# A block of selective scan and FFN on one core: two loads change places, the opening's copies of B and C move to VectorE, and products, a row and an up projection get other slots

## The chip, the cores and the metric

One core of a Trainium2 chip runs the whole program. The metric is the device time of one execution in microseconds (us). The core has five engines that run their own instruction streams in order and meet through semaphores: PE (TensorE, matmuls; PEld is its weight load), DVE (VectorE), ACT (ScalarE), POOL (GpSimd) and SP (SyncE, which here only issues DMAs).

## The reference

```
mod = (silu(c) @ wmod).reshape(1, 6, 1, 256)            # sa, ca, ga, sb, cb, gb
ga, gb = sign(ga) * max(|ga|, 0.25), sign(gb) * max(|gb|, 0.25)
h = layernorm(x) * (1 + ca) + sa                        # x: 2048 tokens x 256
# selective SSM, 16 states n for each of 256 channels, token by token:
dt, B, C = split(h @ x_proj_w.T, [128, 16, 16])
delta = softplus(dt @ dt_proj_w.T + b);  A = -exp(A_log)
state[n] = exp(delta * A[n]) * state[n] + delta * B[n] * h
y = sum over n of state[n] * C[n] + D * h
x = x + ga * y
h = layernorm(x) * (1 + cb) + sb
g = (h @ gate_w.T) * gate_s;  u = (h @ up_w.T) * up_s     # 704 wide, ternary weights
x = x + gb * (((silu(g) * u) @ down_w.T) * down_s)
```

## The kernel before

**Tiling.** The 2048 tokens go in four chunks (c = 0 to 3) of 512. The 256 channels are two halves h of 128 partitions. Step c scans chunk c: 16 slots, one for each state row n, and at slot n the two halves are scanned by DVE (`scan`, L995). I write "scan 2.1" for row 2, half 1. Before a scan ACT makes its decay, exp(delta A), in one of two PSUM banks (`make_decay`, L830), so a decay can be made only when the scan two before it is done. POOL makes the drive of row n, u times B's row, three slots ahead (`drive`, L642); B's rows arrive in pairs in the tiles `brow`, by DMAs that repeat a row of a DRAM scratch (`bc_dram`) on all 128 partitions. Three `brow` buffers serve rows 0 and 1, 2 and 3, 4 and 5, and so on.

**Products.** The state of row n is multiplied by C's row n, one slot later. The table `POOL_C` says which rows POOL does (L654, C's row from a tile `crow` that a DMA filled); the others are DVE's (`times_c`, L969), and for these PE first repeats C's row on 128 partitions in the one PSUM bank `rows_ps` (`spread_row`, L1294). So row by row: DVE's product frees `rows_ps`, PE spreads the next row, DVE can multiply again. PE adds each product into `sums`, three slots behind the scan (`add_state`, L1320), and the D term first of all (`add_dterm`, L1306).

**Beside the scan.** While chunk c is scanned, "F" tasks prepare chunk c + 1 and "K" tasks run the FFN of chunk c - 1. F: statistics of x (st0, st1, agg on DVE), rstd on ACT, nmr (minus mean times rstd) on POOL, xn0 and xn1 on ACT (L713), transposes xT on PE (L1207), hmod0 and hmod1 on ACT (L728), z on PE (L1193), then abs, exp, zb and ln on ACT and delta on DVE; and bc, the product that gives B and C: ACT copies it to `bc_sb` (L752), from where SP stores it to `bc_dram`, and rounds C into `c_parts` (chi, L759), of which DVE takes the rest (clo, L901). K: x2 (`sums` added to x, L895), statistics, h2T, gate0 to gate4, mixed and up0 to up4 on PE (L1241), ACT's gates (L799), one silu over all gates with a table load at each end (L818 to L822), hdn5 and hdn0 to hdn4 on DVE (gates times ups, L942 and L953), and four downs (L1273). "S" tasks are set-up in the opening and in step 0: the last of them fill the weights' bias `wb` and scale the down weights.

**What sets the order.** Lists written by hand give each task a slot: (8.5, "F ln0") is slot 8, behind the second half; -3 means three slots before the step, 16 and over the next step. `FIRST` is for the opening (before step 0) and for chunk 0, `PLAN` for the middle, `CLOSING` for the FFN of chunk 2 during step 3, `FINAL` for that of chunk 3 behind the last scan. `SECOND_LATER` moves the F tasks of chunk 1, which would fall in the opening, by so many slots (2 where it names none). At each slot an engine does its scan, decay or drive, then the products, then its tasks; it never skips ahead, so a task that waits holds all behind it. `PLACE` and its kin give each PE result its PSUM bank; banks 0 to 2 are `side`, 3 is `rows_ps`, 4 and 5 are `decay`.

SP issues in the opening: x of chunk 0, the projection weights, then `load_more`: x of chunk 1 behind a wait for chunk 0's, the FFN weights, the rest of wmod. Behind that come, slot by slot, the stores and loads of B and C and a small DMA that keeps each state's last column.

## Time and profile before

| | |
|---|---|
| median of 3 runs | 316.56 us (315.71 to 316.79) |
| the profiled execution's own time | 314.61 us |
| its span, first to last instruction | 312.8 us |
| lies around the span | 1.8 us |
| DVE busy | 256.8 us, 82% |
| PE busy | 248.9 us, 80% |
| POOL busy | 227.0 us, 73% |
| ACT busy | 183.7 us, 59% |
| mean granted TensorE clock | 0.874 |

Stages of the span: up to 25.4 us the opening (no scan yet), then step 0 up to 84, step 1 up to 146.7, step 2 up to 209.0 and step 3 up to 273.7 us; the rest is the last chunk's FFN. The page divides the span into 40 slices of 7.8 us; each digit is a busy share in tenths, and for PEclk the granted clock in tenths of full speed. A timeline row reads: start (us), duration or, for xN instructions, the time from the first to the end of the last (us), engine, line, operation, written tile <- read tiles, shapes, count, and in brackets how long the engine sat idle just before and whose result ended that.

### The profile page before, as it was taken

How to read it: one execution, taken by the hardware profiler on the slowest of the kernel's cores; microseconds unless marked ns; L12 is line 12 of the kernel's file. 1: busy time of each engine (PE TensorE's matmuls, PEld its weight loads, DVE VectorE, ACT ScalarE, POOL GpSimd, SP SyncE). 2: the span in 40 equal slices, each digit the busy share in tenths (PEclk: the TensorE clock that was granted, in tenths of full speed). 3: DMA queues.
4: the chain of work that ended last, by engine and by line, in shares of the span. 5: the costliest groups of instructions: out<-in, count | busy, mean ns of one | idle time of the engine just before them, and what ended most of it. 6: DMA issues, size and time to landing. Idle time of an engine off the chain costs nothing. (4 is left out here: it accounts for less than half of the span.)

```text
span 312.8 us, 3793 instructions
## 1 busy us (share of the span) xinstructions
PE 248.9 (80%) x1226; PEld 185.5 (59%) x1226; DVE 256.8 (82%) x330; ACT 183.7 (59%) x294; POOL 227.0 (73%) x113
## 2 busy tenths in 40 slices
PE   7876799846387787848889997667899947897995
PEld 7634796435274455635658675446687835685874
DVE  3589966999999899969999999599988959944420
ACT  2688544765845976896349867932464883306400
POOL 1007789999999999979879997995599996700000
PEclk9995559997579889965999999958799995999999
DMA  7916897469262743392524735725636400001002
GB/s 249 327 48 162 156 143 203 69 104 233 73 133 72 137 103 107 72 147 28 124 69 108 161 90 118 135 38 151 167 90 149 118 1 0 2 0 67 2 0 71
DMA packets 33173, 33.09 MB, mean 106 GB/s; under 512 B 14912, under 2 KB 20224, under 8 KB 33152
## 3 DMA queue, kind: packets, MB, share of 16 engines
q1 hardware_dynamic: 32736, 32.01, 44.7%
q10 hardware_dynamic: 416, 0.81, 0.8%
q8 instruction: 12, 0.20, 0.3%
q14 instruction: 9, 0.07, 0.1%
HBM read 30.40 MB, written 2.36 MB: 105 GB/s over the span
## 5 line engine op out<-in xcount | busy, mean ns | idle before, releaser
L642 POOL TENSOR_TENSOR drv<-u,brow 128x1024 f32<-128x1024 f32 x63 | 147.8, 2362 | 21.0 <-DVE u L917 17.1
L830 ACT ACTIVATE decay<-delta,A 128x512 f32<-128x512 f32 x128 | 87.6, 688 | 82.9 <-DVE state L995 81.0
L995 DVE TENSOR_TENSOR_SCAN state<-decay,last,drv 128x512 f32<-128x512 f32 x96 | 119.1, 1268 | 11.7 <-ACT decay L830 11.4
L654 POOL TENSOR_TENSOR drv<-state,crow 128x1024 f32<-128x1024 f32 x29 | 68.7, 2369 | 9.9 <-DVE state L995 9.9
L1320 PE MATMUL sums<-ident,drv 128*128 128x128 f32 x512 | 72.1, 294 | 0.7 <-POOL drv L654 0.5
L1320 PEld LDWEIGHTS sums<-ident,drv 128*128 128x128 f32 x512 | 62.6, 151 | 12.0 <-issue 7.8
L969 DVE TENSOR_TENSOR drv<-state,rows_ps 128x1024 f32<-128x1024 f32 x35 | 41.8, 1195 | 5.4 <-PE rows_ps L1294 5.4
L1241 PE MATMUL side<-h_hi,ffn_hi 128*128 128x512 f32 x76 | 30.0, 479 | 18.6 <-DVE gates L942 16.1
L995 DVE TENSOR_TENSOR_SCAN state<-decay,drv 128x512 f32<-128x512 f32 x32 | 37.5, 1207 | 1.7 <-issue 1.1
L1294 PE MATMUL rows_ps<-c_parts,sel 64*128 64x512 f32 x35 | 19.6, 561 | 22.9 <-DVE drv L969 22.9
L1273 PE MATMUL side<-down_sb,gates 128*128 128x256 f32 x120 | 30.4, 403 | 4.3 <-DVE gates L953 3.5
L1273 PEld LDWEIGHTS side<-down_sb,gates 128*128 128x128 f32 x120 | 22.9, 199 | 10.3 <-issue 7.4
L1241 PEld LDWEIGHTS side<-h_hi,ffn_hi 128*128 128x128 f32 x76 | 14.5, 220 | 24.5 <-issue 23.0
L1241 PE MATMUL side<-h_lo,ffn_hi 128*128 128x512 f32 x76 | 26.5, 433 | 0.0
L1294 PEld LDWEIGHTS rows_ps<-c_parts,sel 64*128 64x128 f32 x35 | 7.2, 206 | 32.5 <-DVE drv L969 27.9
L1241 PEld LDWEIGHTS side<-h_lo,ffn_hi 128*128 128x128 f32 x76 | 16.4, 216 | 4.3
L799 ACT ACTIVATE gates<-side,wb,pack_sb 128x512 f32<-128x512 f32 x18 | 13.6, 768 | 3.3 <-PE side L1241 3.2
L1193 PE MATMUL side<-hmod,W_sb 128*128 128x512 f32 x24 | 11.0, 603 | 3.7 <-ACT hmod L728 3.7
L953 DVE SCALAR_TENSOR_TENSOR gates<-side,wb,gates 128x512 f32<-128x512 f32 x17 | 12.4, 736 | 1.5 <-PE side L1241 1.5
L1257 PE MATMUL decay<-down_sb,gates 128*128 128x256 f32 (+1 forms) x48 | 11.2, 387 | 0.0
L617 POOL TENSOR_TENSOR nmr_K<-negmean_K,rstd_K 128x4 f32<-128x4 f32 x4 | 0.8, 199 | 13.6 <-ACT rstd_K L706 13.6
L1306 PEld LDWEIGHTS sums<-diag_D,hmod 128*128 128x128 f32 x64 | 9.2, 225 | 1.7 <-issue 1.7
(142 smaller groups left out, 291.9 us busy)
## 6 DMA issues: line engine op xcount, KB each, us to landing
brow<-bc_dram SPq DMA_DIRECT2D x31, 512.0 KB, 5.5
crow<-bc_dram SPq DMA_DIRECT2D x13, 512.0 KB, 7.0
resid<-in_x SPq DMA_DIRECT2D x4, 512.0 KB, 5.4
out<-resid SPq DMA_DIRECT2D x8, 256.0 KB, 2.2
gates<-in_wmod ACTq DMA_DIRECT2D x1, 768.0 KB, 6.1
gates<-in_wmod SPq DMA_DIRECT2D x1, 768.0 KB, 8.7
last<-state SPq DMA_DIRECT2D x48, 1.0 KB, 2.5
crow<-bc_dram SPq DMA_DIRECT2D x3, 256.0 KB, 3.7
```

The lines of the kernel that those rows point to most:

```text
L642: nc.gpsimd.tensor_tensor(drv[j % RING_DRV][:, :, 0:S], u[:, c % 2, :, 0:S], b.unsqueeze(1).to_broadcast([P, HALVES, S]), ALU.mult).then_i ...
L654: nc.gpsimd.tensor_tensor(drv[j % RING_DRV][:, :, 0:S], state[j % RING_STATE][:, :, 0:S], row.unsqueeze(1).to_broadcast([P, HALVES, S]), A ...
L799: nc.scalar.activation(gates[:, j, 0:S], src[:, 0:S], ACT.Silu if c == NCH - 1 else ACT.Identity, bias=wb[:, j:j + 1], scale=pack_sb[:, CO ...
L830: nc.scalar.activation(decay[i % RING_DECAY][:, 0:S], delta[:, c % 2, h, 0:S], ACT.Exp, scale=A[:, h * N + n:h * N + n + 1]).then_inc(deca ...
L953: nc.vector.scalar_tensor_tensor(gates[:, j, 0:S], src[:, 0:S], wb[:, FULL + j:FULL + j + 1], gates[:, j, 0:S], ALU.add, ALU.mult).then_in ...
L969: nc.vector.tensor_tensor(drv[j % RING_DRV][:, :, 0:S], state[j % RING_STATE][:, :, 0:S], rows_ps[:, 0:S].unsqueeze(1).to_broadcast([P, HA ...
L995: nc.vector.tensor_tensor_scan(state[j % RING_STATE][:, h, 0:S], decay[i % RING_DECAY][:, 0:S], drv[j % RING_DRV][:, h, 0:S], before, ALU. ...
L1241: ins = nc.tensor.matmul(to[:, 0:S], weights, data, start=part is h2_hi and k == 0, stop=part is h2_lo and k == HALVES - 1)
L1257: ins = nc.tensor.matmul(to[:, b * D:(b + 1) * D], gates[part, j, rows], down_sb[part, j, :], start=j == FULL and b == 0, stop=j == FULL - ...
L1273: nc.tensor.matmul(to, gates[:, j, rows], down_sb[:, j, :], start=j == 0, stop=False)
L1294: nc.tensor.matmul(rows_ps[:, 0:S], sel[:, n:n + 1].to_broadcast([2 * 2 * N, P]), c_parts[:, c % 2, 0:S], start=True, stop=True).then_inc( ...
L1320: ins = nc.tensor.matmul(sums[:, b * D + h * P:b * D + (h + 1) * P], of[:, h, b * P:(b + 1) * P], ident[:, :], is_transpose=True, start=Fa ...
```

## The change

- **Loads.** SP issues the FFN weights ahead of x of chunk 1; the wait for chunk 0's x moves to the weights. DVE's `equal` (does rounding change the weights, L1081, three parts) waits for the first half of the rounded weights only in its first part.
- **Opening's copies.** For chunk 0 the copies bc and chi go from ACT to DVE. Chunks 1 to 3 keep them on ACT.
- **Statistics of x of chunk 1.** `SECOND_LATER` changes: st0, st1 and agg run in step 0 at slots 0.5, 1 and 1 instead of in the opening, rstd at 1.5 instead of 0.5, nmr at slot 2 instead of 0. xn0 and xn1 stay at slots 2 and 2.5.
- **Products.** In steps 1, 2 and 3 two DVE products are done at slots s and s + 0.5 of `SILU_SLOT` (13, 13, 10), for rows s - 2 and s - 1, and the second one's row is spread a slot later. POOL takes row 10 instead of 11 in step 1, and 11 instead of 8 in step 3; step 2 keeps its rows.
- **Step 3.** up2 of chunk 2 goes to slot 11 and to the bank `rows_ps`, up3 and up4 to banks 1 and 0, hdn2 and hdn3 half a slot up. Row 15 is spread at slot 13 (`LAST_ROW`), ahead of down0 and down1, behind a wait for up2's bank.

```diff
-POOL_C = [[4, 6, 9, 11, 13]] + [[1, 3, 5, 7, 9, 11, 13]] * (NCH - 3) + [[1, 3, 5, 6, 7, 10, 13]] + [[1, 2, 4, 5, 7, 8, 10, 12, 13, 14]]
+POOL_C = [[4, 6, 9, 11, 13]] + [[1, 3, 5, 7, 9, 10, 13]] * (NCH - 3) + [[1, 3, 5, 6, 7, 10, 13]] + [[1, 2, 4, 5, 7, 10, 11, 12, 13, 14]]
+SILU_SLOT = [None, 13, 13, 10]
 DVE_C = [[n for n in range(N) if n not in at] for at in POOL_C]
...
-SECOND_LATER = {"st0": -7, "st1": -7, "agg": -7}
+SECOND_LATER = {"st0": 3.5, "st1": 4, "agg": 3.5, "rstd": 3, "nmr": 4}
 FIRST = {
...
-        (7, "F clo"), (8, "F delta0"), (8, "F u0"), (8, "F drive0"), (9, "F delta1"), (9, "F u1"), (9, "F drive1"),
-        (6, "S equal"), (16.5, "S mod2"), (17.5, "S gb"), (22.5, "S wb"), (31, "S same"),
+        (6, "F bc"), (6, "F chi"), (7, "F clo"), (8, "F delta0"), (8, "F u0"), (8, "F drive0"), (9, "F delta1"), (9, "F u1"), (9, "F drive1"),
+        (5, "S equal"), (16.5, "S mod2"), (17.5, "S gb"), (22.5, "S wb"), (31, "S same"),
     ],
...
-        (4, "F abs0"), (4, "F exp0"), (4, "F zb0"), (5, "F bc"), (5, "F chi"), (6, "F ln0"), (6, "F abs1"), (6, "F exp1"), (7, "F zb1"), (7, "F ln1"),
+        (4, "F abs0"), (4, "F exp0"), (4, "F zb0"), (6, "F ln0"), (6, "F abs1"), (6, "F exp1"), (7, "F zb1"), (7, "F ln1"),
...
     "sync": [
-        (1, "S x"), (1, "S ffn"), (1, "S wmod"), (6, "F bc"), (20, "S down"), (26, "S xs"),
+        (1, "S ffn"), (1, "S x"), (1, "S wmod"), (6, "F bc"), (20, "S down"), (26, "S xs"),
     ],
...
-        (11.5, "K hdn5"), (11.5, "K hdn0"), (12, "K hdn1"), (12.5, "K hdn2"), (13, "K hdn3"), (13, "K hdn4"),
+        (11.5, "K hdn5"), (11.5, "K hdn0"), (12, "K hdn1"), (12, "K hdn2"), (12.5, "K hdn3"), (13, "K hdn4"),
...
-        (9, "K up0"), (10, "K up1"), (12, "K up2"), (12, "K up3"), (12, "K up4"),
+        (9, "K up0"), (10, "K up1"), (11, "K up2"), (12, "K up3"), (12, "K up4"),
...
-    "K up0": 0, "K up1": 2, "K up2": 1, "K up3": 0, "K up4": 2, "K down": (1, 2),
+    "K up0": 0, "K up1": 2, "K up2": 3, "K up3": 1, "K up4": 0, "K down": (1, 2),
 }
...
 PLACE_FIRST = {"F xT": (0, 1), "S mod": 3, "F z": (4, 5), "F bc": 2, "F sp": (0, 1)}
+LAST_ROW = 13
 LEAD = 3
...
                 yield kind, name, int(chunk)
+def product_slot(c, n):
+    if SILU_SLOT[c] is None or n not in (SILU_SLOT[c] - 2, SILU_SLOT[c] - 1):
+        return n + KEEP_LAG
+    return SILU_SLOT[c] + (0 if n == SILU_SLOT[c] - 2 else 0.5)
+def row_slot(c, n):
+    if (c, n) == (NCH - 1, N - 1):
+        return LAST_ROW
+    return n + (SILU_SLOT[c] is not None and n == SILU_SLOT[c] - 1)
...
                 elif name == "x":
-                    sp.wait_ge(x_loaded[0], 16)
                     load_x(1)
...
                 elif name == "ffn":
+                    sp.wait_ge(x_loaded[0], 16)
                     for m, w in enumerate((gateT, upT)):
...
                                             ALU.add).then_inc(x2_ready, 1)
+                elif name == "bc":
+                    src, i, k = side_bank(("F bc", c, 0))
+                    dve.wait_ge(side_full[i], k + 1)
+                    nc.vector.tensor_copy(bc_sb[:, 0:S], src[0:2 * N, 0:S]).then_inc(bc_ready, 1)
+                elif name == "chi":
+                    src, i, k = side_bank(("F bc", c, 0))
+                    nc.vector.tensor_copy(c_parts[0:2 * N, c % 2, 0:S], src[0:2 * N, 0:S]).then_inc(chi_ready, 1)
                 elif name == "clo":
...
-                    dve.wait_ge(ffn_hi_ready, HALVES)
                     for to, part in EQUAL:
+                        dve.wait_ge(ffn_hi_ready, 1 if part.stop <= 2 * INTER else HALVES)
                         nc.vector.tensor_tensor(equal_to(to, part), flat(ffn_hi)[:, part].bitcast(F32),
...
                             scan(step, n, h)
-                        for c, m in lagged(step, n, KEEP_LAG) if h == 0 else ():
-                            if m in DVE_C[c]:
-                                times_c(c, m)
+                        for c in (step - 1, step):
+                            for m in DVE_C[c] if 0 <= c < NCH else ():
+                                if c * N + product_slot(c, m) == step * N + n + h / 2:
+                                    times_c(c, m)
                         for task in side_tasks("vector", step, n + h / 2):
...
                     pe.wait_ge(side_free[i], k)
-                if i >= SIDE and use[0][0] == "K":
+                if i >= SIDE and use[0][0] == "K" and use[1] == NCH - 1:
                     pe.wait_ge(scan_done, UNITS * HALVES)
                     pe.wait_ge(prod_dve, rows_upto(NCH))
+                elif i >= SIDE and use[0][0] == "K":
+                    pe.wait_ge(prod_dve, rows_upto(NCH) - 1)
                 return to, side_full[i]
...
                     pe.wait_ge(prod_dve, before)
+                if (c, n) == (NCH - 1, N - 1):
+                    pe.wait_ge(*emptied(("K up2", NCH - 2, 0)))
                 if c == NCH - 2 and n >= BC_SLOT:
...
                 for n in range(N):
-                    spread = 0 <= step < NCH and n in DVE_C[step]
-                    follows = spread and (n - 1) % N in DVE_C[step - (n == 0)]
-                    if spread and not follows:
-                        spread_row(step, n)
+                    rows = [m for m in DVE_C[step] if row_slot(step, m) == n] if 0 <= step < NCH else []
+                    follows = bool(rows) and (rows[0] != n or (n - 1) % N in DVE_C[step - (n == 0)])
+                    if rows and not follows:
+                        spread_row(step, rows[0])
                     for task in side_tasks("tensor", step, n):
                         side_work(*task, full_weights)
-                    ending = step == NCH - 1 and n == N - 1
-                    if spread and follows and not ending:
-                        spread_row(step, n)
+                    if rows and follows:
+                        spread_row(step, rows[0])
                     for c, m in adds_at(step, n):
                         add_state(c, m)
-                    if ending and follows:
-                        spread_row(step, n)
```

On POOL, where the opening ends and step 0 begins; L642 and L659 are the drives of rows 1, 2 and on, L617 and L634 nmr of chunk 0 and then of chunk 1. Before:

```order
L617 TENSOR_TENSOR nmr_F<-negmean_F,rstd_F 128x4
L642 TENSOR_TENSOR drv1<-u,brow0 128x1024
L642 TENSOR_TENSOR drv2<-u,brow1 128x1024
L617 TENSOR_TENSOR nmr_F<-negmean_F,rstd_F 128x4
L642 TENSOR_TENSOR drv3<-u,brow1 128x1024
L642 TENSOR_TENSOR drv4<-u,brow2 128x1024
L642 TENSOR_TENSOR drv5<-u,brow2 128x1024
```

And after, at the same place of POOL:

```order
L634 TENSOR_TENSOR nmr_F<-negmean_F,rstd_F 128x4
L659 TENSOR_TENSOR drv1<-u,brow0 128x1024
L659 TENSOR_TENSOR drv2<-u,brow1 128x1024
L659 TENSOR_TENSOR drv3<-u,brow1 128x1024
L659 TENSOR_TENSOR drv4<-u,brow2 128x1024
L634 TENSOR_TENSOR nmr_F<-negmean_F,rstd_F 128x4
L659 TENSOR_TENSOR drv5<-u,brow2 128x1024
```

Chunk 1's nmr has moved behind the drives of rows 3 and 4, the second of which reads the third brow buffer.

On ACT, start of step 0, before: two decays of row 0, rstd of chunk 1 (L702 to L706), a sum of the weights' comparison (L695), the decays of row 1, and so on to xn0 and xn1 (L713).

```order
L830 ACTIVATE decay<-delta,A 128x512 x2
L702 ACTIVATE logvar_F<-meanvar_F,eps 128x4
L704 ACTIVATE negmean_F<-meanvar_F 128x4
L706 ACTIVATE rstd_F<-logvar_F 128x4
L695 ACTIVATE drv,same<-drv 128x1024
L830 ACTIVATE decay<-delta,A 128x512 x2
L695 ACTIVATE drv,same<-drv 128x1024
L830 ACTIVATE decay<-delta,A 128x512
L713 ACTIVATE xn_F<-resid,nmr_F,rstd_F 128x256 x2
L695 ACTIVATE drv,same<-drv 128x768
L830 ACTIVATE decay<-delta,A 128x512
L713 ACTIVATE xn_F<-resid,nmr_F,rstd_F 128x256 x2
```

And after:

```order
L847 ACTIVATE decay<-delta,A 128x512 x2
L712 ACTIVATE drv,same<-drv 128x1024
L847 ACTIVATE decay<-delta,A 128x512 x2
L719 ACTIVATE logvar_F<-meanvar_F,eps 128x4
L721 ACTIVATE negmean_F<-meanvar_F 128x4
L723 ACTIVATE rstd_F<-logvar_F 128x4
L712 ACTIVATE drv,same<-drv 128x1024
L847 ACTIVATE decay<-delta,A 128x512
L730 ACTIVATE xn_F<-resid,nmr_F,rstd_F 128x256 x2
L712 ACTIVATE drv,same<-drv 128x768
L847 ACTIVATE decay<-delta,A 128x512
L730 ACTIVATE xn_F<-resid,nmr_F,rstd_F 128x256 x2
```

rstd has moved behind the decays of row 1; xn0 still stands between the two decays of row 2, and xn1 ahead of those of row 3.

On PE in step 3, from the end of the ups: L1241 and L1270 are gates and ups, L1273 and L1274 (then L1302 and L1303) the downs, L1320 (L1351) the adds, L1294 (L1325) a spread row. Before:

```order
L1241 MATMUL side<-h_lo,ffn_hi 128x512 x2
L1320 MATMUL sums<-ident,drv 128x128 x16
L1273 MATMUL side<-down_sb,gates 128x256 x5
L1274 MATMUL side<-down_sb,gates 128x256
L1273 MATMUL side<-down_sb,gates 128x256 x5
L1274 MATMUL side<-down_sb,gates 128x256
L1320 MATMUL sums<-ident,drv 128x128 x8
L1294 MATMUL rows_ps<-c_parts,sel 128x512
L1320 MATMUL sums<-ident,drv 128x128 x32
```

And after:

```order
L1270 MATMUL side<-h_lo,ffn_hi 128x512 x2
L1351 MATMUL sums<-ident,drv 128x128 x8
L1325 MATMUL rows_ps<-c_parts,sel 128x512
L1351 MATMUL sums<-ident,drv 128x128 x8
L1302 MATMUL side<-down_sb,gates 128x256 x5
L1303 MATMUL side<-down_sb,gates 128x256
L1302 MATMUL side<-down_sb,gates 128x256 x5
L1303 MATMUL side<-down_sb,gates 128x256
L1351 MATMUL sums<-ident,drv 128x128 x40
```

Row 15 has moved ahead of the downs; five adds follow the downs as before.

## Rows read from the trace of the kernel before

**Rows 1.** The page: DVE and the rest over the span, granted clock in slices

```profile
PE 248.9 (80%) x1226; PEld 185.5 (59%) x1226; DVE 256.8 (82%) x330; ACT 183.7 (59%) x294; POOL 227.0 (73%) x113
...
PEclk9995559997579889965999999958799995999999
```

**Rows 2.** Timeline of ACT, opening and step 0

```profile
14.13 2.64 ACT L689 ACTIVATE ffn_hi<-ffn_sb 128x1408 fp32r<-128x1408 f32 x2 [0.88 <-DMA ffn_sb<-in_upT]
...
18.58 0.57 ACT L752 ACTIVATE bc_sb<-side 32x512 f32<-32x512 f32 x1
...
30.30 1.09 ACT L713 ACTIVATE xn_F<-resid,nmr_F,rstd_F 128x256 f32<-128x256 f32 x2 [0.24 <-POOL nmr_F L617]
...
32.13 0.67 ACT L830 ACTIVATE decay<-delta,A 128x512 f32<-128x512 f32 x1
32.74 1.08 ACT L713 ACTIVATE xn_F<-resid,nmr_F,rstd_F 128x256 f32<-128x256 f32 x2
...
41.56 0.76 ACT L728 ACTIVATE hmod<-side,gmod 128x512 f32<-128x512 f32 x1
...
52.02 0.69 ACT L765 ACTIVATE splus<-side,pack_sb 128x512 f32<-128x512 f32 x1 [3.62 <-PE side L1193]
```

**Rows 3.** Timeline of DVE, opening and step 0

```profile
16.80 3.23 DVE L1081 TENSOR_TENSOR drv<-ffn_hi,ffn_sb 128x1024 f32<-128x1024 f32 x3 [1.09 <-ACT ffn_hi L689]
...
20.35 0.68 DVE L901 TENSOR_TENSOR c_parts<-side,c_parts 32x512 fp32r<-32x512 f32 x1
...
35.05 2.33 DVE L995 TENSOR_TENSOR_SCAN state<-decay,drv 128x512 f32<-128x512 f32 x2
...
38.41 2.33 DVE L995 TENSOR_TENSOR_SCAN state<-decay,drv 128x512 f32<-128x512 f32 x2
43.10 1.22 DVE L969 TENSOR_TENSOR drv<-state,rows_ps 128x1024 f32<-128x1024 f32 x1 [2.36 <-PE rows_ps L1294]
```

**Rows 4.** DMAs issued from 22 to 23 us: size, us from issue to landing

```profile
crow<-bc_dram SPq DMA_DIRECT2D x1, 512.0 KB, 8.9
brow<-bc_dram SPq DMA_DIRECT2D x1, 512.0 KB, 12.6
```

**Rows 5.** Timeline of POOL, start of step 0: nmr, drive of row 3, row 4

```profile
30.07 0.20 POOL L617 TENSOR_TENSOR nmr_F<-negmean_F,rstd_F 128x4 f32<-128x4 f32 x1
30.22 2.36 POOL L642 TENSOR_TENSOR drv<-u,brow 128x1024 f32<-128x1024 f32 x1
34.91 9.30 POOL L642 TENSOR_TENSOR drv<-u,brow 128x1024 f32<-128x1024 f32 x4 [2.33 <-DMA brow<-bc_dram]
```

**Rows 6.** Timeline of PE, step 0: transposes xT, row 3, D term

```profile
37.17 1.97 PE L1207 MATMUL side<-ident,xn_F 128*128 128x128 f32 x8
...
42.27 0.79 PE L1294 MATMUL rows_ps<-c_parts,sel 64*128 64x512 f32 x1
42.99 3.62 PE L1306 MATMUL sums<-diag_D,hmod 128*128 128x128 f32 x16
```

**Rows 7.** Timeline of ACT ahead of silu, steps 1 and 2

```profile
128.82 0.69 ACT L830 ACTIVATE decay<-delta,A 128x512 f32<-128x512 f32 x1 [0.92 <-DVE state L995]
...
195.72 0.69 ACT L830 ACTIVATE decay<-delta,A 128x512 f32<-128x512 f32 x1 [0.50 <-DVE state L995]
```

**Rows 8.** Timeline of DVE: scans behind silu in steps 1, 2, 3; row 11's product

```profile
138.60 2.46 DVE L995 TENSOR_TENSOR_SCAN state<-decay,last,drv 128x512 f32<-128x512 f32 x2 [2.42 <-ACT decay L830]
...
202.75 2.46 DVE L995 TENSOR_TENSOR_SCAN state<-decay,last,drv 128x512 f32<-128x512 f32 x2 [3.58 <-ACT decay L830]
...
256.44 2.46 DVE L995 TENSOR_TENSOR_SCAN state<-decay,last,drv 128x512 f32<-128x512 f32 x2 [3.37 <-ACT decay L830]
...
261.58 1.19 DVE L969 TENSOR_TENSOR drv<-state,rows_ps 128x1024 f32<-128x1024 f32 x1
```

**Rows 9.** Timeline of PE, end of step 3: first down, last four adds

```profile
267.86 2.40 PE L1273 MATMUL side<-down_sb,gates 128*128 128x256 f32 x10 [0.83 <-issue]
...
275.24 3.71 PE L1320 MATMUL sums<-ident,drv 128*128 128x128 f32 x32
```

## The prediction

> **What bounds the kernel now.** I read the page first [rows 1]: DVE is busy for 256.8 of 312.8 us, more than any other engine, so I asked of each stretch what DVE waits for. From 25 to 273 us DVE scans, and its timeline has idle time in four places only: in step 0, where PE or ACT is late, and once in each of steps 1, 2 and 3, behind silu [rows 8]. Anything that moves DVE's scans outside these gaps moves the end. Then I looked at who sets DVE's pace in step 0. DVE's product of row 3 waited 2.36 us for PE's row [rows 3]. PE had been busy without a break since before xT at 37.17, through row 3 at 42.27 and the D term at 42.99 [rows 6], at half the granted clock: the page's PEclk is 5 in its fourth to sixth slice (23.5 to 46.9 us) [rows 1]. ACT then waited 3.62 us for PE's z, with the decays of row 7 queued behind it [rows 2]. So from xT on, PE's chain (xT, row 3, D term, z) carries step 0, and whoever delays xT delays the kernel. Behind the last scan the chain of PE's downs and adds ends at 275.24 + 3.71 = 278.95, and x2 starts on it [rows 9].
>
> **The change, part by part.**
>
> *Loads.* ACT waited 0.88 us for the FFN weights before it rounded them at 14.13 [rows 2]. With x of chunk 1 out of the way this wait can go, between 0 and 0.88; I take all of it, since the transfer put behind is 512 KB and ACT's earlier work then binds. The second half of the weights is rounded at 13.25 + 2.64 = 15.89.
>
> *Opening on DVE.* The first of three comparisons moves into DVE's gap of 1.09 us ahead of 16.80, the other two take two thirds of 3.23 us [rows 3] and end at 15.89 + 2.15 = 18.0. The copies bc and chi on DVE do not stand in the trace; their nearest row is clo, the same 32x512 tile out of PSUM, 0.68 us on DVE [rows 3], and the lower bound is ACT's 0.57 [rows 2]. I take 0.65: bc is ready at 18.7, where ACT had it at 18.58 + 0.57 = 19.15, and clo can start at 19.4 instead of 20.35. So the store of B and C leaves 0.5 us earlier and the first scan starts about 1 us earlier. ACT saves the two copies, which nothing on this path needs.
>
> *Statistics and nmr.* Here the gain is lost again. Before, nmr of chunk 1 ran at 30.07 between the drives of rows 2 and 3, and xn0 followed at 30.30 [rows 5, 2]. Now nmr is queued behind the drives of rows 3 and 4, as the order shows. The drive of row 4 had to wait for its brow buffer, and began at 34.91 after 2.33 us of idle time [rows 5]. That buffer was issued just past 22 us and took 12.6 us, the crow pair issued right before it 8.9 us [rows 4]: the broadcast loads land one after the other, these two 3.7 us apart, so they come 0.5 us earlier because the store does, and no more. Row 4's drive then begins at 34.4, takes 9.30 / 4 = 2.33, nmr 0.20, and xn0 begins at 37.0 instead of 30.30. xn0 stands on ACT between the two decays of row 2, and a decay cannot be made ahead, since there are two banks. From xn0's start to that decay's start it is 32.13 - 30.30 = 1.83 us and to xn1's end 32.74 + 1.08 - 30.30 = 3.52 [rows 2]. So scan 2.1 starts at 37.0 + 1.83 + 0.7 = 39.5 instead of 35.05 [rows 3], and xn1 ends at 40.5.
>
> From there two paths run to the D term on PE. By xT: 40.5 instead of 37.17, 3.35 later, and row 3 with it at 45.6. By DVE: decay 3.0 waits behind xn1 and comes at 41.1 (scan 3.0 was at 36.2, half-way in the pair at 35.05); from scan 3.0 to scan 3.1 it was 38.41 - 36.2 = 2.2 us, so scan 3.1 starts at 43.3; from scan 3.1 to the end of hmod1 it was 41.56 + 0.76 - 38.41 = 3.91 [rows 2, 3], so hmod1 ends at 47.3. The D term needs both, and starts at 47.3 instead of 42.99 [rows 6]: **4.3 us later**. Behind it PE's order is as before, up to z, on which ACT and the decays of row 7 wait. DVE has no idle time between there and silu of step 1 to take any of it back. The statistics themselves (about 1.8 us on DVE, now between scans 0.1 and 1.1) are already covered: DVE is ready with the products of rows 0 to 2 before the delayed scans.
>
> Of this chain, the landing is the term I know least. Its bounds: if the buffer is there when row 3's drive ends (30.22 + 2.36 [rows 5] less the 0.5 and nmr's 0.2, 31.9), all from nmr on comes 2.5 us earlier than worked out above and the D term is 1.8 late; if the loads land as late as before, or half a us later for the copies' sake, it is 4.9.
> The Trainium skill ("DMA: Bandwidth & Descriptors", Queues, rings and completion order) says that each DMA engine consumes the descriptors of a ring in order. By that rule, the trace agrees (8.9 us, then 12.6 us for two loads issued within a us), row 4's buffer cannot overtake the three loads ahead of it.
>
> *Silu in step 1.* POOL takes row 10, DVE's row 10 product (1.1 us ahead of scan 11.1) is gone, and row 11's is done at slot 13. From the decay at 128.82, which waited 0.92 us for scan 11.1 [rows 7], ACT works without a break through two gates and three decays to silu. It can start there at 127.8, when the gate before it ends, so silu and all behind it come **1.0 us** earlier. DVE then has row 12's product in its stall of 2.42 us [rows 8], which is covered: 1.4 stays for 1.1 of work. If the gap were all that counts one would book 1.2.
>
> *Silu in step 2.* The rows stay; row 11's product moves from ahead of scan 12.1 to behind scan 13.0. The only thing that it frees is the decay of scan 13.1, which waited 0.50 us at 195.72 [rows 7]: behind it ACT goes straight into silu. Gain **0.6 us** (the wait and its hand-over), not the product's 1.2, though DVE's stall of 3.58 [rows 8] has room for it.
>
> *Silu in step 3.* Ahead of silu ACT is busy without a break, so silu starts when it did; DVE's added row 8 fits in the 3.37 us [rows 8]. No gain, no loss. Behind silu row 11's product at 261.58 (1.19 us, 1.11 from start to start) [rows 8] goes to POOL, which has given row 8 away. So hdn4 ends 1.1 earlier.
>
> *Row 15 and up2.* The downs wait for hdn4, so they start at 266.75 instead of 267.86. Behind them PE did one add, row 15's spread and four adds in a row, the last four in 3.71 us [rows 9]; now five adds without the spread: 0.42 less. x2 starts at 278.95 - 1.1 - 0.4 = 277.4: **1.5 us** earlier. Row 15's product, which waited for its row, no longer decides: it finds its row spread and is done while the adds still run. up2 in rows_ps waits for row 9's product and runs in silu's time, at no cost; up3 then needs hdn5 only. The last chunk's FFN follows x2 unchanged.
>
> *Sum.* + 4.3 - 1.0 - 0.6 - 1.5 = + 1.2 us. On the profiled execution's 314.6 us (span 312.8) that gives 315.8; this execution lies 1.95 below the median of 316.56, and I forecast for the median: **317.8 us**.
>
> **Rivals.**
>
> *The rows come in time.* If brow's third buffer lands when row 3's drive ends, step 0 loses 1.8 instead of 4.3, and the sum is 1.8 - 3.1 = -1.3: 315.3, faster. It decides at a landing of 33.2 us: any earlier and the change gains. Against it stand 8.9 and 12.6 us from issue to landing [rows 4]; for it, that the loads start half a us earlier.
>
> *The delay is swallowed.* DVE's 2.36 us wait for row 3 [rows 3] and ACT's 3.62 us for z [rows 2] look like slack. They are PE's time, and PE is what is delayed, so I give this little. It would leave the three gains: 316.56 - 3.1 = 313.5.
>
> *The clock stays low.* PE gets idle time ahead of xT and ahead of the D term that it did not have, and the granted clock was at its lower level, 1.2 GHz, until 46.9 at least in the page's slices. The D term took 3.62 us [rows 6] at that level. If the rise to 2.4 GHz comes later by one such stretch against PE's work, PE runs some 4 us of work at half speed and loses 2: 319.8. The Trainium skill ("TensorE: Matmul & The Clock Gate", Part 1) calls the lower clock the default, which activity lifts and idleness brings back. By that rule the new idle time speaks for this rival.
>
> *Silu does not start earlier.* If PE's gates or POOL hold ACT ahead of silu, the 1.0 and 0.6 fall away, and x2's 1.5 stays: 4.3 - 1.5 = + 2.8, 319.4.
>
> **Numbers.** The forecast has a chance of 0.50, the early rows 0.15, the swallowed delay 0.11, the low clock 0.13, silu not earlier 0.11. The range holds the first rival and the last two: 315.0 to 320.2 us. A measurement of this kernel can tell about 0.3%, 0.95 us, from no change. My forecast is 1.2 above with an uncertainty of about that size, so 0.20 of its 0.50 lie within. Faster by over 0.3%: 0.11 + 0.10 = 0.21; within: 0.20 + 0.04 + 0.01 = 0.25; slower: 0.30 + 0.13 + 0.11 = 0.54.
>
> **What would show it.** In the profile after: nmr of chunk 1 on POOL near 36.7 us, behind an idle wait for brow; xn0 on ACT near 37 after about 4 us of idle time; scan 2.1 near 39.5; the D term near 47.3. If nmr is there before 35, the landing was wrong. Silu's stall on DVE shrinks to under 1.5 us in step 1 and near 1.8 in step 2, and scan 14.0 of step 1, less the delay of step 0, comes 1.0 earlier. x2 of chunk 2 starts 21.0 us behind the first scan past silu of step 3, where it was 278.95 - 256.44 = 22.5. The forecast is wrong as a whole if the D term starts before 45.

## The result, and the profile after

The changed kernel takes 319.29 us (median of 7 runs, 318.21 to 320.14); the kernel before, run beside it, 316.56 (7 runs, 315.70 to 317.43). The ratio is 1.0087, with a 95% interval of 1.006 to 1.0113: **slower, by about 2.7 us, under 1%.** The forecast was 317.8 in a range of 315.0 to 320.2. Medians here and below are of all runs, while ratios and their intervals leave out runs over 1.5% above the fastest of the same kernel, so the two can differ by some tenths of a per cent. The profiled execution took 319.1 us, with a span of 317.2 against 312.8 before.

The page of the kernel after, busy time over the span and granted clock in slices:

```profile
PE 256.6 (81%) x1226; PEld 191.7 (60%) x1226; DVE 258.2 (81%) x332; ACT 183.0 (58%) x292; POOL 227.4 (72%) x113
...
PEclk9795557995659979985799999759599995998999
```

Against [rows 1], ACT gave DVE two instructions (294 to 292, 330 to 332), and no other count of instructions moved between engines. PE issues the same 1226 instructions and is busy 7.7 us longer: it is slower, not busier. The digits say where: against before, the second and the seventh slice are 7 where they were 9, the 29th is 5 where it was 7, and the 37th is 8 where it was 9.

Step 0 shows what was forecast. POOL's timeline, kernel after:

```profile
28.59 4.66 POOL L659 TENSOR_TENSOR drv<-u,brow 128x1024 f32<-128x1024 f32 x2 [0.75 <-DMA brow<-bc_dram]
35.00 2.36 POOL L659 TENSOR_TENSOR drv<-u,brow 128x1024 f32<-128x1024 f32 x1 [1.75 <-DMA brow<-bc_dram]
37.31 0.21 POOL L634 TENSOR_TENSOR nmr_F<-negmean_F,rstd_F 128x4 f32<-128x4 f32 x1
```

and ACT, DVE and PE of the same stretch, in the order of the chain:

```profile
37.55 1.09 ACT L730 ACTIVATE xn_F<-resid,nmr_F,rstd_F 128x256 f32<-128x256 f32 x2 [3.15 <-POOL nmr_F L634]
40.09 1.22 DVE L1020 TENSOR_TENSOR_SCAN state<-decay,drv 128x512 f32<-128x512 f32 x1 [2.82 <-ACT decay L847]
41.13 1.97 PE L1236 MATMUL side<-ident,xn_F 128*128 128x128 f32 x8 [1.76 <-ACT xn_F L730]
46.23 0.79 PE L1325 MATMUL rows_ps<-c_parts,sel 64*128 64x512 f32 x1
46.95 3.78 PE L1337 MATMUL sums<-diag_D,hmod 128*128 128x128 f32 x16
54.54 3.70 PE L1222 MATMUL side<-hmod,W_sb 128*128 128x512 f32 x8
56.56 0.69 ACT L782 ACTIVATE splus<-side,pack_sb 128x512 f32<-128x512 f32 x1 [4.19 <-PE side L1222]
```

Row 4's drive waited 1.75 us for its buffer (2.33 in [rows 5]) and nmr stood behind it: 37.31 instead of 30.07. xT begins 3.96 us later than in [rows 6], the D term 3.96, and ACT's splus, which waits for z, 4.54 later than in [rows 2].

DVE's timeline at the three scans behind silu, and at the end of step 3:

```profile
142.43 2.46 DVE L1020 TENSOR_TENSOR_SCAN state<-decay,last,drv 128x512 f32<-128x512 f32 x2 [1.39 <-ACT decay L847]
...
205.99 2.46 DVE L1020 TENSOR_TENSOR_SCAN state<-decay,last,drv 128x512 f32<-128x512 f32 x2 [2.99 <-ACT decay L847]
...
260.86 2.46 DVE L1020 TENSOR_TENSOR_SCAN state<-decay,last,drv 128x512 f32<-128x512 f32 x2 [2.27 <-ACT decay L847]
...
277.04 1.22 DVE L994 TENSOR_TENSOR drv<-state,rows_ps 128x1024 f32<-128x1024 f32 x1
281.70 1.22 DVE L912 TENSOR_TENSOR resid<-resid,sums 128x1024 f32<-128x1024 f32 x1 [3.44 <-PE sums L1351]
```

With x2 of each chunk (the addition `resid<-resid,sums` on DVE) and these scans as milestones, the span divides so. "Opening alone" is the third kernel of the next section.

| from, to | before | after | difference | opening alone |
|---|---|---|---|---|
| start, first scan | 25.36 | 25.79 | **+ 0.43** | 24.26 |
| first scan, x2 of chunk 0 | 66.54 | 70.94 | + 4.40 | 71.23 |
| x2 of chunk 0, scan behind silu of step 1 | 46.70 | 45.70 | - 1.00 | 46.72 |
| to x2 of chunk 1 | 17.03 | 17.02 | 0 | 17.02 |
| to the scan behind silu of step 2 | 47.12 | 46.54 | - 0.58 | 47.12 |
| to x2 of chunk 2 | 17.02 | 17.02 | 0 | 17.02 |
| to the scan behind silu of step 3 | 36.67 | 37.85 | **+ 1.18** | 36.64 |
| to x2 of chunk 3 | 22.55 | 20.84 | - 1.71 | 22.55 |
| to the end | 33.8 | 35.5 | **+ 1.7** | 33.9 |
| span | 312.8 | 317.2 | + 4.4 | 316.5 |

The losses and gains that were forecast are there: + 4.8 up to x2 of chunk 0, and - 1.0, - 0.6, - 1.7. The three numbers in bold are not in the prediction, which had the first scan 1.0 us earlier and the other two unchanged. For the + 1.18, DVE's timeline has the addition of the first downs in step 3. Before, it ran at 227.73 after 1.38 us of idle time; now

```profile
232.01 0.69 DVE L985 TENSOR_TENSOR resid<-resid,side 128x512 f32<-128x512 f32 x1 [2.42 <-PE side L1303]
```

and PE's timeline shows why it is late, in the downs and in the first matmuls of the last chunk's FFN:

```profile
223.24 4.60 PE L1302 MATMUL side<-down_sb,gates 128*128 128x256 f32 x10 [3.30 <-DVE gates L978]
227.77 1.22 PE L1303 MATMUL side<-down_sb,gates 64*128 64x256 f32 x2
228.92 2.43 PE L1302 MATMUL side<-down_sb,gates 128*128 128x256 f32 x10
...
290.38 1.22 PE L1270 MATMUL rows_ps<-h_hi,ffn_hi 128*128 128x512 f32 x2 [1.49 <-ACT h_hi L762]
291.40 1.05 PE L1270 MATMUL rows_ps<-h_lo,ffn_hi 128*128 128x512 f32 x2
292.25 1.05 PE L1270 MATMUL decay<-h_hi,ffn_hi 128*128 128x512 f32 x2
```

Ten downs took 4.60 us and then, the same ten, 2.43; the first gate's matmuls took 1.22 and 1.05 where before they took 0.73 and 0.80. The rows differ in nothing but the granted clock. The view of windows says so directly (window; its length, busy us of PE, PEld, DVE, ACT, POOL with counts, PEclk, DMA share, GB/s), kernel after:

```profile
9.00:14.00 5.00, 5.00 (x29) 4.81 (x29) 1.21 (x10) 2.73 (x6) 0.00 (x0) 0.66 1.02 356
...
46.00:50.00 4.00, 4.00 (x17) 3.55 (x17) 3.21 (x4) 2.41 (x4) 1.60 (x2) 0.50 0.43 127
...
290.00:294.00 4.00, 3.62 (x9) 2.90 (x10) 1.19 (x2) 1.11 (x2) 0.00 (x0) 0.57 0.00 0
```

In the kernel before the same three windows have 1.00, 0.96 and 1.00.

### The profile page after: what moved, and what is told of

It reads as the page before. It is cut to its first block and busy times, and to the rows that moved or that the text cites. A ratio compares the mean times of both kernels' runs of the same rounds, so it can differ in the third digit from the quotient of the medians.

```text
span 317.2 us, 3794 instructions
## 1 busy us (share of the span) xinstructions
PE 256.6 (81%) x1226; PEld 191.7 (60%) x1226; DVE 258.2 (81%) x332; ACT 183.0 (58%) x292; POOL 227.4 (72%) x113
## 5 line engine op out<-in xcount | busy, mean ns | idle before, releaser
L659 POOL TENSOR_TENSOR drv<-u,brow 128x1024 f32<-128x1024 f32 x63 | 148.1, 2373 | 20.5 <-DMA brow<-bc_dram 20.4
L1351 PE MATMUL sums<-ident,drv 128*128 128x128 f32 x512 | 74.7, 301 | 0.0
L1351 PEld LDWEIGHTS sums<-ident,drv 128*128 128x128 f32 x512 | 65.4, 156 | 11.6 <-issue 8.8
L1325 PE MATMUL rows_ps<-c_parts,sel 64*128 64x512 f32 x35 | 20.5, 586 | 28.1 <-DVE drv L994 28.1
L1270 PE MATMUL side<-h_hi,ffn_hi 128*128 128x512 f32 x74 | 29.6, 486 | 9.6 <-DVE gates L967 5.8
L1302 PE MATMUL side<-down_sb,gates 128*128 128x256 f32 x120 | 30.9, 408 | 4.1 <-DVE gates L978 4.1
L1325 PEld LDWEIGHTS rows_ps<-c_parts,sel 64*128 64x128 f32 x35 | 7.5, 214 | 38.5 <-DVE drv L994 33.6
L1302 PEld LDWEIGHTS side<-down_sb,gates 128*128 128x128 f32 x120 | 23.2, 202 | 10.4 <-issue 7.4
L1270 PE MATMUL side<-h_lo,ffn_hi 128*128 128x512 f32 x74 | 26.6, 445 | 0.0
L1270 PEld LDWEIGHTS side<-h_hi,ffn_hi 128*128 128x128 f32 x74 | 14.1, 221 | 15.0 <-issue 13.6
L1270 PEld LDWEIGHTS side<-h_lo,ffn_hi 128*128 128x128 f32 x74 | 16.4, 222 | 4.3
L1159 PE MATMUL side<-mod,ffn_sb 128*128 128x1 f32 x44 | 8.4, 320 | 3.1 <-DVE gbds L1100 3.1
L1159 PEld LDWEIGHTS side<-mod,ffn_sb 128*128 128x128 f32 x44 | 8.4, 294 | 3.6 <-DVE gbds L1100 3.6
```

The source lines that it names most:

```text
L659: nc.gpsimd.tensor_tensor(drv[j % RING_DRV][:, :, 0:S], u[:, c % 2, :, 0:S], b.unsqueeze(1).to_broadcast([P, HALVES, S]), ALU.mult).then_i ...
L1159: ins = nc.tensor.matmul(to[:, j:j + 1], ffn_sb[:, k, j * P:(j + 1) * P], mod[:, 6 + k:7 + k], start=k == 0, stop=k == HALVES - 1)
L1270: ins = nc.tensor.matmul(to[:, 0:S], weights, data, start=part is h2_hi and k == 0, stop=part is h2_lo and k == HALVES - 1)
L1302: nc.tensor.matmul(to, gates[:, j, rows], down_sb[:, j, :], start=j == 0, stop=False)
L1325: nc.tensor.matmul(rows_ps[:, 0:S], sel[:, n:n + 1].to_broadcast([2 * 2 * N, P]), c_parts[:, c % 2, 0:S], start=True, stop=True).then_inc( ...
L1351: ins = nc.tensor.matmul(sums[:, b * D + h * P:b * D + (h + 1) * P], of[:, h, b * P:(b + 1) * P], ident[:, :], is_transpose=True, start=Fa ...
```

## The experiments

Ratios are to the kernel before, run beside each; times of different kernels are compared by their ratios, since its own median moved from 315.6 to 316.6 between sessions. Places in the span are read from one profiled execution of each kernel. The long edits are given by what they take over from which kernel.

**The opening alone.** The kernel before with the new `FIRST` and `SECOND_LATER`, the swapped loads and the DVE copies, and nothing of steps 1 to 3.

> The kernel before with only the opening of the changed one. By the prediction's term of 4.3 us for the opening and step 0: 320.9. By the trace of the changed kernel, whose step 1 began 4.5 us later: 321.1. The rival, a delay that is swallowed in steps 1 to 3: 318 or less. The first scan should start within 0.5 us of 25.4, if the early start that was forecast (24.4) does not come; at 24.4, if it was the clock of one execution that took it away.

Measured: 318.61 us, ratio 1.0108 (1.0061 to 1.0155). Slower, by less than expected. The table's last column shows how the loss travels: x2 of chunk 0 comes 3.59 us later than before, and every milestone behind it up to x2 of chunk 3 is 3.57 to 3.61 later, the span 3.7. Nothing between step 0 and the end takes any of it back, which was the prediction's ground for calling the delay unswallowed. The first scan is at 24.26, as forecast (24.4), 1.1 us better than before, and the D term is at 45.55, 2.56 late instead of 4.3. The early first scan is the exception: of the four kernels with loads, copies and statistics all changed, the other three (the changed kernel and two below) have it at 25.79, 26.03 and 26.68, with PE at half clock in a stretch between 10 and 19 us; of the five with the whole old opening four have it at 24.78 to 25.58 and one at 28.50. Such a stretch also came with the loads alone, and once (the 28.50) with the old opening, so nothing here lays it to the edit.

**All but the opening.** The changed kernel with the old opening.

> The changed kernel with the opening of the kernel before (loads, copies on ACT, statistics of chunk 1 in the opening, comparisons behind both halves); the changes of steps 1, 2 and 3 stay. By the sum of the prediction these are worth 1.0 + 0.6 + 1.5 = 3.1 us: 313.5. The trace of the changed kernel showed 1.0, 0.6 and 1.7 at their places, but 1.0 us given back at x2's downs in step 3 and 1.4 us in the last chunk's ups, both times with PE at half clock where it had been at full. If this loss belongs to the changes of steps 1 to 3, the time is 316.56 - 3.3 + 2.4 = 315.7; if it is a matter of the single execution, 313.3.

Measured: 315.17 us, ratio 0.9952 (0.9912 to 0.9992), - 1.5 us. The forecast had - 3.1 for this part. Its profiled execution is the longest of its ten, 318.75 us. In it the first scan is at 28.50, behind half clock from 10.4 to 20.6 us, and from x2 of chunk 2 to the scan behind silu it takes 39.65 us, with 10 us of half clock at the downs.

**nmr ahead of row 4's drive.**

```
-SECOND_LATER = {"st0": 3.5, "st1": 4, "agg": 3.5, "rstd": 3, "nmr": 4}
+SECOND_LATER = {"st0": 3.5, "st1": 4, "agg": 3.5, "rstd": 3, "nmr": 3}
```

> The changed kernel with chunk 1's nmr one slot earlier on POOL: behind row 3's drive, ahead of row 4's. In the changed kernel xn0 began at 37.55 us, row 4's drive at 35.00 behind 1.75 us of idle time, scan 2.1 at 40.09, xT at 41.13 and the D term at 46.95 (42.99 before). Theory 1, nmr queued behind row 4's drive holds ACT: nmr comes at 33.3, xn0 at 33.6, scan 2.1 follows row 1's product at 37.2, xT follows row 2 on PE at 39.3, the D term comes at 45.1, and the time falls by 1.9 us to 317.4. Theory 2, what delays step 0 is only the statistics on DVE ahead of the down weights' scale (gbds was ready at 35.0 instead of 32.9): xT stays where it is, and the time stays at 319.3.

Measured: 315.56 us, ratio 0.9945 (0.9909 to 0.9981). One instruction of 0.2 us, one slot earlier in POOL's queue, takes the whole loss away. Whether the kernel is then faster than before is less sure: the median of all ten runs is 315.56 against 315.71 for the kernel before. POOL and ACT of this kernel:

```profile
33.60 0.20 POOL L634 TENSOR_TENSOR nmr_F<-negmean_F,rstd_F 128x4 f32<-128x4 f32 x1
35.86 9.29 POOL L659 TENSOR_TENSOR drv<-u,brow 128x1024 f32<-128x1024 f32 x4 [2.06 <-DMA brow<-bc_dram]
```
```profile
34.58 1.07 ACT L730 ACTIVATE xn_F<-resid,nmr_F,rstd_F 128x256 f32<-128x256 f32 x2
```

ACT's 3.15 us of idle time are gone, and z starts at 52.29 instead of 54.54, 2.25 us earlier. Part of the difference in span, 314.2 against 317.2, is not nmr's: in this execution the last chunk's FFN ran at full clock (33.8 us to the end instead of 35.5).

The first scan comes at another time in each execution, so the price of step 0 is best read as the distance from it to the D term. That is 17.6 us in all ten profiles with the statistics at their old place, 19.3 here, and 21.2, 21.3 and 21.0 in the three kernels with nmr at its late slot. So nmr's slot costs about 1.8 us of the 3.5. The other 1.7 is there with nmr early too, and PE's timeline shows its path, before and then in this kernel (`gbds`, the down weights' scale that DVE makes, feeds 16 matmuls that stand ahead of xT):

```profile
32.94 3.58 PE L1130 MATMUL side<-mod,ffn_sb 128*128 128x1 f32 x16 [2.04 <-DVE gbds L1075]
```
```profile
35.31 3.57 PE L1159 MATMUL side<-mod,ffn_sb 128*128 128x1 f32 x16 [3.09 <-DVE gbds L1100]
39.53 1.97 PE L1236 MATMUL side<-ident,xn_F 128*128 128x128 f32 x8
```

The statistics stand on DVE ahead of `gbds`; PE waits for it and then has no idle time up to xT.

**Chunk 1's statistics put back, loads and copies kept.**

```
-SECOND_LATER = {"st0": 3.5, "st1": 4, "agg": 3.5, "rstd": 3, "nmr": 4}
+SECOND_LATER = {"st0": -7, "st1": -7, "agg": -7}
```

> The changed kernel with only the places of chunk 1's statistics, rstd and nmr put back: statistics in the opening, nmr at slot 0; loads and copies stay as changed. If the 4.5 us of step 0 come from these places, they go, and the statistics now stand ahead of the copies of B and C: the first scan near 26.3 us, the D term near 43.9, the time 319.3 - 4.0 + 0.9 = 316.2 or less. If the loads or DVE's copies were to blame, the D term stays above 46 and the time at 319.

Measured: 315.11 us, ratio 0.9967 (0.9938 to 0.9995). xn0 is at 30.83 and z at 50.49, 4.05 earlier than in the changed kernel, and the D term is 17.6 us behind the first scan, as before. But the first scan is at 25.57, later than the 25.36 of before: the loads and copies gain nothing here. DVE's timeline of this kernel:

```profile
14.39 3.36 DVE L1106 TENSOR_TENSOR drv<-ffn_hi,ffn_sb 128x1024 f32<-128x1024 f32 x3 [0.15 <-ACT ffn_hi L706]
17.67 1.40 DVE L900 BATCH_NORM_STATS2 stats_F<-resid 128x6 f32<-128x256 f32 x4
18.99 0.66 DVE L918 COPY bc_sb<-side 32x512 f32<-32x512 f32 x1
```

The statistics stand ahead of the copy. Three more kernels with this opening, below, have the first scan at 25.55 to 25.64. So the copy on DVE can pay only where the statistics have left, and they leave at the price of DVE time in step 0.

**Loads alone.** The kernel before with the FFN weights ahead of the second x, and each comparison waiting for its own half.

> The kernel before with the loads alone swapped: FFN weights ahead of the second x, and the equal copies waiting for their own half. The run with all of the opening's edits had the first scan at 24.26 us against 25.36. By the prediction's terms: the 0.88 us wait of the first rounding goes and the two copies of ACT, which stay on ACT, come 0.9 us earlier, so the first scan is at 24.5 and the copies on VectorE are worth 0.2 of the 1.1 us. Rival: without the copies moved the chain of ACT (splus, delta) is what releases them, and the first scan is at 25.0 or later. One look: the instants of the opening decide, not the time.

The first scan is at 25.38 (one run, 316.48 us). That is not the 24.5 expected, but it doesn't refute it either: the product W took 1.91 us here (1.03 before), at half clock, and W_sb on DVE came at 13.81 instead of 12.60. How the 1.1 us divide between loads and copies stays open.

**The three silu edits apart.** Each on the kernel before, with the old opening: step 3's (`SILU_SLOT = [None, None, None, 10]`, row 15, up2, POOL's rows of chunk 3), step 1's (`[None, 13, None, None]` with POOL's row 10), step 2's (`[None, None, 13, None]`).

> The kernel before with the edit of step 3 alone: product 8 of the last chunk goes ahead of silu's wait, up2 and row 15 ahead of the downs, Pool takes other rows; opening and steps 1 and 2 as before. In the four earlier runs that hold this edit, the part from the first scan behind silu to the last chunk's x2 took 20.84 us against 22.55, but the part ahead of it (x2 of the third chunk to the scan behind silu) took 37.9 to 39.7 us against 36.7, and half clock at the downs there lasted 6 us or more against 3. Theory A, that lateness belongs to the silu edit of step 2: here that part is 36.6 to 36.8, the later one 20.8, and the time falls by 1.7 us, ratio 0.9945. Theory B, it belongs to the edit of step 3 itself: that part is 37.8 or more, ratio 0.998 or above.

> The kernel before with the edit of step 1 alone: one product moved ahead of silu's wait, its row one slot later, Pool's row 11 given to VectorE and row 10 to Pool. Forecast: x2 of the first chunk to the scan behind silu 45.7 us against 46.7, all else as before: ratio 0.997. Rival: the clock at the downs of step 2 or 3 changes too, and 1 us or more comes back: ratio 1.000 or above.

> The kernel before with the edit of step 2 alone: product 11 or 12 of that chunk moved ahead of silu's wait, its row one slot later. Forecast in the prediction: 0.6 us off the wait, ratio 0.998. Theory A (the late clock at step 3's downs belongs to this edit): x2 of the third chunk to the next scan behind silu takes 37.8 us or more against 36.7, so the sum is 0.6 to 1 us slower, ratio 1.002 to 1.003. Theory B: that part stays at 36.7, ratio 0.998.

| edit | ratio (95%) | median | its own part of the span | x2 of chunk 2 to the scan behind silu |
|---|---|---|---|---|
| step 3 | 0.9958 (0.9912 to 1.0004) | 315.14 | 20.85 against 22.55 | 36.75 |
| step 1 | 0.9953 (0.9928 to 0.9978) | 314.25 | 45.67 against 46.70 | 34.98 |
| step 2 | 1.0002 (0.9962 to 1.0042) | 316.97 | 46.50 against 47.12 | **38.27** |

The kernel before beside them has a median of 315.62. Each edit gains in its own part what was measured in the changed kernel, 1.7, 1.0 and 0.6. Only step 1's is clear of noise in time. Step 2's alone gives its gain back, in step 3, where theory A had it.

**The change without statistics moved and without step 2's edit.**

```
-SECOND_LATER = {"st0": 3.5, "st1": 4, "agg": 3.5, "rstd": 3, "nmr": 4}
+SECOND_LATER = {"st0": -7, "st1": -7, "agg": -7}
-SILU_SLOT = [None, 13, 13, 10]
+SILU_SLOT = [None, 13, None, 10]
```

> The changed kernel with chunk 1's statistics put back where they were (as in the second-old run) and with step 2's product put back as well. Theory A: against that run (span 312.8 us) the part from x2 of the third chunk to the scan behind silu falls from 38.4 to 36.7, and step 2, where that run had no gain (47.3 us against 47.1 before), loses nothing: span 311.1, ratio 0.992. Theory B: no difference from that run, ratio 0.997.

Measured: 312.86 us (10 runs), ratio **0.9914** (0.9875 to 0.9954), span 311.1, with 36.74 us from x2 of chunk 2 to the scan behind silu. This version beats both kernels. The windows at the downs of step 3, of this kernel

```profile
219.00:222.00 3.00, 2.12 (x7) 1.73 (x8) 2.96 (x6) 0.69 (x1) 2.36 (x1) 0.75 0.92 173
222.00:225.00 3.00, 3.00 (x9) 1.78 (x8) 2.96 (x9) 1.23 (x4) 0.47 (x2) 0.68 0.86 167
225.00:228.00 3.00, 3.00 (x16) 2.17 (x15) 1.67 (x3) 2.91 (x6) 3.00 (x2) 1.00 0.48 145
```

and of step 2's edit alone:

```profile
219.00:222.00 3.00, 1.84 (x7) 1.65 (x8) 2.97 (x6) 0.69 (x1) 2.36 (x1) 0.90 0.84 168
222.00:225.00 3.00, 3.00 (x7) 1.53 (x6) 2.96 (x8) 1.22 (x4) 0.18 (x2) 0.50 0.91 173
225.00:228.00 3.00, 3.00 (x8) 2.37 (x8) 1.51 (x2) 2.63 (x5) 3.00 (x3) 0.50 0.65 154
```

In both the clock falls within 2 us of the downs' start at 220, but in one PE is back at full clock at 223 to 224, in the other at 228.

**The addition of the downs one slot later.** The addition that waits in step 3 goes behind two more scans and a product, so that slow downs have time; with step 2's edit out, with it in, and in the changed kernel itself.

```
-        (19, "K out0"), (22, "K out1"),
+        (20, "K out0"), (22, "K out1"),
```

> The kernel of f4 (chunk 1's statistics and step 2's product back, the rest of the change kept) with the addition of the first downs in step 3 one slot later on VectorE and SyncE: two scans and a product stand ahead of it now. In f4 that addition waited 1.33 us on TensorE's downs. Theory (the downs reach the end of the kernel through this one wait): the 1.33 us go, x2 of the third chunk to the scan behind silu 35.4 us against 36.7, span 309.8, ratio 0.987. Rival: the product behind the two scans needs a row that stands behind the same downs, or the bank comes free later and the next downs are late: 36.0 us or more, ratio 0.990.

> As g1, but with step 2's product moved ahead of silu's wait as in the changed kernel. By the theory the long half clock at the downs (6 us against 3) is then still in the trace and costs VectorE nothing or the 0.3 us that the row is late: x2 of the third chunk to the scan behind silu 35.4 to 35.8 us, 0.6 us gained in step 2, span 309.5, ratio 0.986. Rival: the slow downs still hold the row and through it the product: 36.7 us or more, ratio 0.990.

> The changed kernel itself with that addition one slot later. It waited 2.42 us there. Theory: that wait goes, x2 of the third chunk to the scan behind silu 35.5 us against 37.85, time 2.4 us less than the changed kernel's 319.3: 316.9, ratio 1.001 to the kernel before. Rival as in g1: 318 or more, ratio 1.005.

Measured: ratios 0.9913 (0.9847 to 0.9979), 0.9910 (0.9838 to 0.9982) and 1.0081 (1.0017 to 1.0145); x2 of chunk 2 to the scan behind silu 35.35, 37.83 and 39.59 us. The theory that one wait hands the slow downs on falls. In the last kernel that wait is gone, and two others are there:

```profile
234.76 1.22 DVE L994 TENSOR_TENSOR drv<-state,rows_ps 128x1024 f32<-128x1024 f32 x1 [1.74 <-PE rows_ps L1325]
...
245.09 0.69 DVE L985 TENSOR_TENSOR resid<-resid,side 128x512 f32<-128x512 f32 x1 [2.60 <-PE side L1303]
```

PE's row for the product stands behind the same downs, as the rival had it, and the second addition is late in turn. In the first of the three, PE was at full clock at these downs and the wait was gone for that reason too, so it does not tell the edit's worth; in time it is no better than the kernel without it (0.9913, 0.9914). The edit is worth nothing that these runs show.

Over the 14 profiles (both kernels and twelve experiments), x2 of chunk 2 to the scan behind silu goes with how long PE stays at half clock at these downs: 34.98 and 35.35 us with no half clock, 36.6 to 36.8 with about 3 us of it (five kernels), 37.8 to 38.4 with 6 to 7 us (five), 39.59 and 39.65 with 10. The seven kernels with step 2's edit are all at 37.8 or above, the seven without it all at 36.8 or below. That is one profile each. In time the picture is weaker: with and without the edit, the pair on the statistics put back is 0.9967 against 0.9914 with intervals that just overlap, and the pair on the later addition 0.9910 against 0.9913. That the longer half clock comes with step 2's edit is shown in the traces; how the edit brings it, and what it costs on average, stays open.

## Why the prediction was right, and where its sum was off

*Who sets the pace of step 0.* Right. xT, row 3, the D term and z carry it, and the opening alone moves every later milestone by the same 3.6 us. The swallowed delay (313.5) is excluded.

*The size of that delay.* The D term moved by 3.96 us where 4.3 was forecast, and that closeness is luck: two errors offset each other. The first scan was to come 1.0 us earlier and came 0.43 later; from it to the D term it was to take 22.9 us and took 21.2 (17.6 before). In the opening alone, where the first error is absent, the D term is 2.56 us late; about 1.0 more comes between it and x2 of chunk 0.

*The landing.* The wait was right, and it held nmr. Row 4's drive began at 35.00 (34.4 forecast; by the prediction's sum 33.2 or earlier would have reversed the sign). DMAs issued from 23.0 to 24.5 us, kernel after (size, us to landing):

```profile
crow<-bc_dram SPq DMA_DIRECT2D x1, 512.0 KB, 8.9
brow<-bc_dram SPq DMA_DIRECT2D x1, 512.0 KB, 11.0
```

One lands behind the other in both kernels; that a load can't overtake another is more than that shows. Their distance was not as fixed as I had it: 3.7 us plus 0.5 at issue in the kernel before, 2.1 plus 1.4 now. In the opening alone row 4's drive began at 33.60, 1.3 us earlier than before for a B and C ready 0.5 earlier. The rest of the chain, from nmr to row 3, came as forecast and 0.5 to 0.7 us late, which is the landing's own 0.6.

*The D term.* "The D term needs both", xT and hmod1, is wrong. This D term is chunk 0's and reads chunk 0's hmod, which ACT had made by 13.9 us; the hmod1 on its way is chunk 1's, for z. ACT's timeline, kernel after:

```profile
12.28 1.63 ACT L745 ACTIVATE hmod<-side,gmod 128x512 f32<-128x512 f32 x2 [2.20 <-DVE gmod L1059]
...
47.09 0.77 ACT L745 ACTIVATE hmod<-side,gmod 128x512 f32<-128x512 f32 x1
```

The D term started at 46.95, at once behind row 3 and ahead of that hmod1. Without the false condition the forecast would have been 46.3, the loss 3.3 instead of 4.3, and the sum + 0.2.

*Loads, and the opening on DVE.* The steps were right, the clock was not in them. ffn_hi no longer waits (13.81 us), bc and chi take 0.67 us each (0.65 forecast), and at full clock the first scan is at 24.26 in the opening alone. In the changed kernel's profiled execution it is at 25.79. There PE ran at half clock from 10.5 to 13.9 us (xT 1.95 us, where it was 1.07, W 1.57 where it was 1.03), and W_sb on DVE, with DVE's queue behind it, came at 14.43 instead of 12.60.

*The statistics.* "Already covered" held for the changed kernel only because nmr was late: xT still waited 1.76 us for xn. The prediction looked at DVE's products and not at `gbds`, by which the statistics reach PE. With nmr one slot earlier, 1.7 us of them are left (19.3 against 17.6 us from the first scan to the D term).

*Silu in steps 1 and 2.* Right: 1.00 (1.0) and 0.58 (0.6), and 1.03 and 0.62 with each edit alone. (In three of the kernels above, nmr ahead, statistics back, and that without step 2's edit, the addition of step 2's second downs waited 0.7 us near 181 and the part ahead of step 2's silu is 0.7 to 0.8 longer; in others with the same instructions there it didn't.) That silu does not start earlier is excluded. One number beside it was wrong: the stall of step 2 was to shrink to 1.8 us and is 2.99. The product moved from ahead of one scan to ahead of the next, both in front of the stall, and I had counted it as added to the stall; only silu's 0.6 came off.

*Row 15 and up2.* Right: 20.84 us from the scan behind silu to x2 (21.0 forecast), row 15's product without a wait.

*Silu in step 3: "no gain, no loss".* Wrong as a statement on the stretch ahead of it, by + 1.18 us. The step that failed is the one that didn't look at the downs of step 3, 30 us ahead: their addition waited 2.42 us instead of 1.38.

*"The last chunk's FFN follows x2 unchanged".* Its instructions did, and took 1.7 us more: half clock from 290.4 to 293.8. Three other kernels of the 14 have such a stretch (35.2 us to the end), the others take 33.8 to 34.1, with the same instructions. It came in kernels with the new opening and with the old one, so nothing here lays it to the change.

*The sum.* Between the profiled executions it was + 4.4, not + 1.2: + 0.5 in the opening and step 0, + 1.2 ahead of silu in step 3, + 1.7 at the end, - 0.2 on the other terms. The 1.2 and the 1.7 come with PE at half clock; the 0.5 is what is left of the two errors above and of what comes behind the D term. The median was missed by 1.5 only, since I added the 1.2 to a median that itself lay 1.95 above its profiled execution: such stretches were in it already. In time, the opening alone gave + 3.4 us (4.3 forecast) and all but the opening - 1.5 (- 3.1 forecast), so in this sum too one part's error makes up for some of the other's. The rival "the clock stays low" named a price of 2.0 and gave 319.8. Its place was seen too, with PE at 0.50 until 51.5 us instead of 46.3: the three kernels with the late nmr have 27.3 us of half clock there, all others 23.9. But the D term to z took 7.59 us against 7.01, and it takes 7.0 to 8.1 in the kernels with the old places, so no price can be read from that; the larger pieces lay elsewhere. The forecast's mechanism decided the sign. The size of the loss is as much the half clock's.

## What to carry to other kernels

A small instruction that one engine makes for another has to be placed by what stands ahead of it in its queue at that time: 0.2 us of nmr behind a drive that waited for a DMA cost 1.8 us. When a task is moved, every result that stands behind it in its new queue moves too: the statistics reached PE by the down weights' scale, which the prediction didn't follow. And a forecast that comes out near may hold two errors that offset each other, so each term is checked by itself. A gain that is read from one profile is worth the clock of that profile; a sum of gains of 0.6 to 1.7 us has to be set beside stretches of half clock that come and go with 1 to 3 us each, and tested part by part, because one part of four (step 2's edit) gave nothing and one (the statistics) cost more than all others brought. Where the end was carried by a wait on one engine's results, moving the waiting instruction later showed the next instructions that waited for the same engine.
